# x's lower half turned on TensorE in the place of idle turns, moved waits, and two branches split in four, in a four-layer graph network

## What is computed

```python
x = _layernorm(x + L0(x)); x = _layernorm(x + L1(x)); x = _layernorm(x + L2(x)); x = _layernorm(x + L3(x))
# L0: adj[src, dst] = adj[dst, src] = 1 (a set, not a sum), plus the identity, scaled by deg**-0.5 from both
#     sides; adj @ (x @ weight) + bias
# L1: three convolutions h = A @ (h @ W) + b, where A counts each edge as often as it stands (plus loops)
#     and is scaled by deg**-0.5 from both sides
# L2: q = x @ Wq + bq, k = x @ Wk + bk, v = x @ Wv + bv; a = q @ k.T / sqrt(D), -1e6 where there is no
#     edge; softmax(a) @ v
# L3: h = relu(A @ (x @ W1) + b1); out = A @ (h @ W2) + b2
```

## Time and profile before

| | |
|---|---|
| median of three runs | 546.02 us |
| the profiled execution | 545.62 us |
| its span, first to last instruction | 543.8 us |
| granted clock of TensorE, mean | 0.999 |
| TensorE busy with products | 529.8 us, 97% (2317 instructions) |
| TensorE's weight loads | 373.1 us, 69% |
| VectorE busy | 398.3 us, 73% |
| ScalarE busy | 171.7 us, 32% |
| GpSimd busy | 143.1 us, 26% |

### The profile page before, as it was taken

One profiled execution on the slowest core, in us unless ns is written; L12 is line 12 of the kernel. 1 busy time (PEld: TensorE's weight loads), 2 busy tenths in 40 slices (PEclk: granted clock), 3 DMA queues, 4 the chain that ended last, 5 costly groups with the idle time before them and its releaser, 6 DMA issues.

```text
span 543.8 us, 7062 instructions
## 1 busy us (share of the span) xinstructions
PE 529.8 (97%) x2317; PEld 373.1 (69%) x2317; DVE 398.3 (73%) x873; ACT 171.7 (32%) x361; POOL 143.1 (26%) x135
## 2 busy tenths in 40 slices
PE   8999999999999999999999999899989999999995
PEld 6555565357788888888674764467678888888643
DVE  6888888789878989355576977897887916690165
ACT  5999896472021022220220000542343100120200
POOL 3000000085228504022224800653400390000021
PEclk9999999999999999999999999999999999999999
DMA  8724000100102012000000000000020300000012
GB/s 290 272 79 153 3 1 0 42 1 0 41 9 107 2 19 79 0 1 0 2 1 0 2 0 0 1 0 1 2 77 0 136 0 1 1 1 0 1 58 99
DMA packets 12763, 20.19 MB, mean 37 GB/s; under 512 B 3243, under 2 KB 3507, under 8 KB 12726
## 3 DMA queue, kind: packets, MB, share of 16 engines
q1 hardware_dynamic: 12726, 19.69, 10.7%
HBM read 17.57 MB, written 2.11 MB: 36 GB/s over the span
## 4 chain that ended last, share of the span: by engine, by line
PE 83%; DVE 8%; ACT 4%; issue 3%; POOL 1%; DVEq 0%; POOLq 0%; ACTq 0%
PE bank L951 13%; PE bank L770 13%; PE bank L955 12%; PE bank L788 11%; PE bank L1011 9%; PE bank L844 4%; PE bank L658 3%; PE bank L697 3%; PE bank L643 3%; PE bank L662 3%; PE bank L666 3%; PE bank L983 1%; DVE wk_rows L1519 1%; PE bank L674 1%; ACT apart L1101 1%
## 5 line engine op out<-in xcount | busy, mean ns | idle before, releaser
L549 POOL TENSOR_TENSOR rstd<-veps,mhalf 128x1 f32<-128x1 f32 x32 | 22.2, 695 | 177.5 <-DVE veps L1450 174.7
L1370 DVE TENSOR_TENSOR count<-bank,count 128x160 f32 x128 | 41.3, 323 | 13.9 <-PE bank L697 7.2
L788 PE MATMUL bank<-adj,y_hi 128*128 128x512 f32 x128 | 51.1, 399 | 0.0
L788 PE MATMUL bank<-adj,y_lo 128*128 128x512 f32 x128 | 50.4, 394 | 0.0
L1457 DVE SCALAR_TENSOR_TENSOR xs<-bank,dinv,xs 128x512 f32<-128x512 f32 x23 | 16.9, 746 | 43.9 <-PE bank L844 30.5
L1101 ACT ACTIVATE apart<-col_lo,edge_key 128x128 bf16<-128x128 int16 x128 | 44.0, 395 | 0.7 <-PE bank L686 0.7
L586 POOL TENSOR_SCALAR mask<-count 128x1024 bf16<-128x1024 uint16 x8 | 23.5, 2931 | 52.3 <-DVE peak L1669 43.5
L1354 DVE TENSOR_TENSOR hot_key<-col_key,key 128x320 bf16<-128x320 int16 x128 | 35.4, 316 | 0.2 <-issue 0.2
L697 PEld LDWEIGHTS bank<-hot_key,lo_near 128*128 128x128 bf16 x128 | 12.0, 100 | 31.8 <-issue 23.4
L658 PE MATMUL bank<-w_sb,x0t 128*128 128x512 f32 x64 | 33.1, 601 | 0.6 <-ACT x0t L1082 0.3
L1108 ACT ACTIVATE lo_far<-apart,ones 128x256 bf16<-128x256 bf16 x64 | 31.9, 500 | 0.0
(11 more groups left out here) (288 smaller groups left out, 1241.2 us busy)
## 6 DMA issues: line engine op xcount, KB each, us to landing
w_sb<-in_L_gnn_W_dram SPq DMA_DIRECT2D x3, 1024.0 KB, 5.6
xs<-in_x_dram SPq DMA_DIRECT2D x2, 1024.0 KB, 7.1
v_sb<-in_L_gnn_W_dram SPq DMA_DIRECT2D x2, 1024.0 KB, 6.0
out_dram<-xs SPq DMA_DIRECT2D x7, 256.0 KB, 2.0
w_sb<-in_L_gnn_weight_dram SPq DMA_DIRECT2D x4, 256.0 KB, 6.1
wq_sb<-in_L_gnn_Wq_dram SPq DMA_DIRECT2D x1, 1024.0 KB, 10.6
wk_sb<-in_L_gnn_Wk_dram SPq DMA_DIRECT2D x1, 1024.0 KB, 12.8
wq_rows<-in_L_gnn_Wq_dram SPq DMA_DIRECT2D x1, 1024.0 KB, 7.8
```

The costliest lines, as they stand in the source:

```text
L788: mm = pe.matmul(to, y[part][:, k, f * P:(f + 1) * P], m[:, k, half], start=n == 0 and part == 0 and m is mat, stop=n == NB - 1 and part = ...
L1370: return V.tensor_tensor(count[:, :, bass.ds(at_dst, WIN)], bank[:, slot, n * KEYS:(n + 1) * KEYS].rearrange("p (h d) -> p h d", h=NB), co ...
```

## The change

Four idle turns and eight idle turns go from the opening; in the place of the eight stand the first eight pieces (`TURNED_FIRST`), which are transposes of x's lower half. `EARLY` is three products and sixteen turns, and the pieces of the first "xw" unit stand in another order: its first three products, then the eight turns, then the fourth product. `turn_links(h)` waits for `unit_out` for h = 0, 1 and 2, each for the unit that had its own bank, where h = 0 waited for all. The two If/Else that held whole layers become four, around `cols_steps(2)`, the four `rows_step`s (`layer1_rows`), `cols_steps(10)` and `cols_steps(12)`; the fourteen products of kind "f", those of kind "h" and the last weight products stand between or behind them and are in the program once, not twice. In attention the first score product M1 of pair 2 stands ahead of `turn_probs(0)` on TensorE, `exponents(1)` ahead of `first_part("s", 2)` on ScalarE, `quotients(6)` ahead of `first_mix(2)` on ScalarE, and `reciprocal(6)` ahead of `add_m57(1)` on VectorE.

```diff
--- before.py
+++ after.py
@@ -33,7 +33,8 @@
 WIN = 20
 PAIR = 2
 BY_DVE = 2
-EARLY = 20 * 200 + 2 * 1024
+EARLY = 16 * 200 + 3 * 1024
+TURNED_FIRST = 8
 SHARE = 1280
 TURNED = 200
 SLOTS = 4
@@ -313,7 +314,7 @@
             elif kind == "xw":
                 turns = [(m, k) for m in (n - 2, n - 1) for k in range(4)]
                 if n == 6:
-                    ORDER += [(n, 0), (n, 1)] + turns[:6] + [(n, 2)] + turns[6:] + [(n, 3)]
+                    ORDER += [(n, k) for k in range(3)] + turns + [(n, 3)]
                 else:
                     for k in range(4):
                         ORDER += turns[2 * k:2 * k + 2] + [(n, k)]
@@ -343,7 +344,7 @@
         UA = max(n for n, _ in ORDER[:ALONG]) + 1
         BEHIND = [m for m in range(ALONG, len(ORDER) - 4) if ORDER[m][0] <= UA]
         REST = [m for m in range(ALONG, len(ORDER) - 4) if ORDER[m][0] > UA]
-        assert len(BEHIND) + len(REST) == len(ORDER) - 4 - ALONG and len(REST) == NB
+        assert len(BEHIND) + len(REST) == len(ORDER) - 4 - ALONG and len(REST) == NB and UA % 4 == 3
 
         def unit_bank(n):
 
@@ -686,7 +687,8 @@
                     mm = pe.transpose(bank[:, 2 + n // 2, at_col:at_col + G],
                                       key_rows[:, n, c * P:(c + 1) * P], ident[0:G, 0:G])
                 mm.then_inc(rows_turned, 1)
-            idle_turns(8)
+            for m in range(TURNED_FIRST):
+                piece(m)
             pe.wait_ge(rows_set, 2)
             pe.matmul(bank[:, 0, 0:2 * SPANS * G], ones[0:G, :], group_dia[:].rearrange("g a b -> g (a b)"),
                       start=True, stop=True).then_inc(rows_turned, 1)
@@ -698,8 +700,7 @@
                                  start=c % PAIR == 0, stop=c % PAIR == PAIR - 1)
 
 
-            idle_turns(4)
-            for m in range(*pieces[-1]):
+            for m in range(TURNED_FIRST, pieces[-1][1]):
                 piece(m)
             for g in range(G):
                 pe.wait_ge(win_added, max(2, g + 3 - SLOTS))
@@ -731,8 +732,8 @@
 
             def turn_links(h):
 
-                if h == 0:
-                    pe.wait_ge(unit_out, UA + 1)
+                if h < 3:
+                    pe.wait_ge(unit_out, UA - 2 + h)
                 if h >= 3:
                     pe.wait_ge(sym_max, h - 2)
                 to = bank[:, HALF + h % 3, :].bitcast(BF16)
@@ -955,21 +956,24 @@
                         mm = pe.matmul(to, a[:, k, n * P:(n + 1) * P], b[:, k, :], start=k == 0, stop=k == 1)
                 mm.then_inc(part_done, 1)
 
-            def layer1(mats):
-                more = mats[1] if len(mats) > 1 else None
-                cols_steps(2, adj, yb, NB, more)
-                for n in range(FOLDED):
-                    part(*PARTS[n])
+            def whole_or_apart(steps, rest):
+
+                with pe.If(big < 1):
+                    steps(None)
+                with pe.Else():
+                    steps(rest)
+
+            def layer1_rows(more):
+
                 for half in range(2):
                     rows_step(4 + half, adj, ya1, 2 * NB, more, order=PAIRS)
                 for half in range(2):
                     rows_step(6 + half, adj, yb1, 3 * NB, more)
 
-            with pe.If(big < 1):
-                layer1([adj])
-            with pe.Else():
-                layer1([adj, rest_l1])
-
+            whole_or_apart(lambda more: cols_steps(2, adj, yb, NB, more), rest_l1)
+            for n in range(FOLDED):
+                part(*PARTS[n])
+            whole_or_apart(layer1_rows, rest_l1)
 
             def turn_probs(m):
 
@@ -1027,8 +1031,9 @@
                 for m in names:
                     mix(p, m)
 
+            scores(2, ("M1",))
             turn_probs(0)
-            scores(2, ("M1", "M2", "M6"))
+            scores(2, ("M2", "M6"))
             turn_probs(1)
             mixes(0, ("M1", "M4"))
             scores(2, ("M7", "M5"))
@@ -1054,21 +1059,19 @@
             mixes(2, ("M5", "M7", "M3"))
             mixes(3, MIXES)
 
-            def layer3(mats):
-                more = mats[1] if len(mats) > 1 else None
+            def layer3_first(more):
+
+                if more is not None:
+                    pe.wait_ge(rest_set, 2)
                 cols_steps(10, adj, y3, 4 * NB, more, TILES)
-                for n in range(IN_LAYER2, len(PARTS)):
-                    part(*PARTS[n])
-                cols_steps(12, adj, y3, 5 * NB, more, PAIRS)
-                pe.wait_ge(w_in["v2"], 16)
-                for half in range(2):
-                    weight_step(14 + half, half, by_cols(gt3), v2_sb, 12 + half)
-
-            with pe.If(big < 1):
-                layer3([adj])
-            with pe.Else():
-                pe.wait_ge(rest_set, 2)
-                layer3([adj, rest_l3])
+
+            whole_or_apart(layer3_first, rest_l3)
+            for n in range(IN_LAYER2, len(PARTS)):
+                part(*PARTS[n])
+            whole_or_apart(lambda more: cols_steps(12, adj, y3, 5 * NB, more, PAIRS), rest_l3)
+            pe.wait_ge(w_in["v2"], 16)
+            for half in range(2):
+                weight_step(14 + half, half, by_cols(gt3), v2_sb, 12 + half)
 
         @block.scalar
         def _(act):
@@ -1255,8 +1258,8 @@
             exponents(0)
             quotients(0)
             copy_probs(0)
+            exponents(1)
             first_part("s", 2)
-            exponents(1)
             quotients(1)
             copy_probs(1)
             first_mix(0)
@@ -1275,8 +1278,8 @@
             quotients(5)
             copy_probs(5)
             exponents(6)
+            quotients(6)
             first_mix(2)
-            quotients(6)
             exponents(7)
             copy_probs(6)
             quotients(7)
@@ -1821,8 +1824,8 @@
             m3("s", 3)
             mask_scores(6)
             m4("s", 3)
+            reciprocal(6)
             add_m57(1)
-            reciprocal(6)
             add_m3(1)
             mask_scores(7)
             all_sums(2)
```

## The result

| | before | changed |
|---|---|---|
| median of six runs | 545.81 us | 548.56 us |
| lowest, highest | 545.48, 546.28 | 547.84, 555.24 |
| ratio | | 1.0068, 95% interval 1.0042 to 1.0095 |

Forecast were 546.5 and a range of 542.9 to 547.7. The profiled execution is the slowest of the six, 555.24 us with a span of 553.4, so it shows more than a usual run has to pay. The other five took 547.84 to 549.45.

A forecast was written before the change was run, and what follows sets the result against it. TensorE was taken as nearly always at work, so only its pauses could be saved. Opening 0.5, links 0.7, scores -0.1, tile 6 1.45 and branches -3.0 gave -0.45: 546.5 us at the median, 8-in-10 range 542.9 to 547.7.

The forecast's parts named there:

- Opening: Start and counting: twelve idle turns go, TensorE gets ahead until VectorE limits it; 0.5 us gained, bounds 0 and 1.3.
- what VectorE itself gains: Counting groups 3 and 7, where VectorE now waits for TensorE: 0.2 us of the opening's gain stays.
- x's half could land late: Opening: each 0.1 of late landing delays the counting 0.1, up to 0.5; no separate chance, inside the forecast's range.
- turn_links: First link transposes: no wait for wfold's copy, link slices late next; 0.7 us gained, bounds 0.6 and 0.84.
- Scores: First score product ahead of turn_probs(0): wait moves to turn_probs(1), quotient slightly later; -0.1 us, bounds -0.2 and +0.7.
- Tile 6: turn_probs(6) in attention: earlier quotient lets it start when TensorE is free; 1.45 us gained, bounds 1.1 and 1.6.
- Next late is M1 of pair 3: Behind tile 6: M1's bank is freed by add_m57(2), which comes only 1.1 to 1.5 us earlier.
- Branches: Jumps at 183, 266, 456, 511: code-block pauses cost 1.2, 0.2, 1.6 and 0 us; sum -3.0.
- The new jumps stand where data transfers are few: New jumps: the prediction's argument against the rival that code arrives later.
- Sum: Whole kernel: all terms come to -0.45 us, giving 546.5 at the median, no change that can be told.
- Short jumps cost nothing: New jumps: skipping some 517 instructions, they reach code perhaps held already; gains of 2.35 stand, 543.6 us; chance 0.27.
- Slower: code arrives later: Block behind each target: later code delays 183, 266, 456, perhaps 511; 547.9 us at 0.45 delay; chance 0.17.

The follow-up runs named there:

- e1_again: The changed kernel run once more without an edit: 549.58 us, ratio 1.0077.
- h1_scores_back: e4_shift with the old order at the first scores on TensorE and ScalarE, new opening kept: 543.41 us, ratio 0.9953.
- e4_shift: The changed kernel plus 42 harmless waits in TensorE's stream, moving the four jump targets behind a block's edge: 544.04 us, ratio 0.9969.
- e2_u_later: The changed kernel with SyncE's u_rows transfer held back until four products behind the first new jump are done: 549.19 us, ratio 1.0067.
- h4_u_later_again: e2_u_later run once more without an edit: 548.98 us.
- h2_before_shift: The kernel before with nothing but the 42 extra waits added: 544.32 us, ratio 0.9970.
- h3_two_moves: h2_before_shift plus the links' waits and the moves of quotients(6) and reciprocal(6), both If/Else whole: 542.80 us, ratio 0.9943.
- g1_best: e4_shift with the opening and the first scores' order of the kernel before: 542.91 us, ratio 0.9941.

## Why the prediction was wrong, step by step

- **Opening, forecast 0.5 gained: wrong, and of the wrong sign.** It moved 1.3 us of idle turns out, and the counting ended 0.2 us later (0.28 by the pair above). The lead of TensorE was there at group 0; what I took to stay was "what VectorE itself gains", 0.2, and that came: its adding at group 8 is 0.25 us earlier in e1_again and stays so up to group 48. The other 0.3, from "work moved behind groups 16, 22, 38 and 45", did not. The waits for hot_key rose from 0.6 us in two places to 1.2 to 1.4 in three, and where TensorE is the limit again it had no lead. That x's half could land late stood among the rivals, inside the range; it came in three profiles of nine. The loss is the traces' finding: in time the kernels with and without the new opening have intervals that overlap.
- **turn_links, forecast 0.7: right in kind, 0.3 to 0.5 in size.** The eight transposes do follow the slices, and take 0.80 us for 0.62.
- **Scores, forecast -0.1: right in place, wrong in price.** The wait moved to turn_probs(1), 1.90 us, inside "1.5 to 2", and up to there the changed kernel had lost 0.1 on the kernel before (+9.22 to +9.32). What I did not look for is what lies behind it, the 0.4 us at tile 3 or 1.65 of half clock. The order costs 0.9 us by the ratios of h1_scores_back and e4_shift (intervals that overlap) and about 0.7 by the four profiles without a slow stretch.
- **Tile 6, forecast 1.45: right, 1.3 in size.** The lag fell from 9.95 us ahead of tile 6 to 8.28, and rose again to 8.66 by layer 3, most of that at M1 of pair 3, as the prediction had it ("Next late is M1 of pair 3"). Putting it back cost 1.2 to 1.9.
- **Branches, forecast -3.0: right in place; in size between right and 1.3 short.** Three long jumps more, pauses after so many products and none at the fourth: as drawn. Forecast were three products ahead of the first pause, three ahead of the second and eight turns; four, seven and nine ran. By my recount I had counted labels of the listing as instructions, which they are not; without them the distances are 8, 15 and 22. No run tests that, but the products and turns that ran fit it. Over the old pause the pauses delayed the later work by 2.4 us in e2_u_later and 2.7 in h4_u_later_again (1.9 and 2.2 of it idle time), less than the 3.0. What failed is that a pause was priced at its length: behind the first of them stood a stretch at half clock in three of four profiles, 1.7 to 2.5 us more. "The new jumps stand where data transfers are few" failed too: u_rows was in flight at the first.
- **Sum: the step that failed.** The forecast had the gains at 2.55 us; together they came to 0.1 to 0.3 (e4_shift beside h2_before_shift). Two gains stood, links and tile 6, at 1.5 of their 2.15 (from h2_before_shift to h3_two_moves). The opening and the order at the scores, which I had at +0.4, cost 1.1 to 1.5 (from e4_shift to g1_best): these two terms are most of the miss. The branches cost 4.5 to 5.9 us against the same kernel without pauses; less the old pause's 1.6 or 1.7 that is 2.9 to 4.3 for the 3.0 forecast. With gains of 0.1 and the low end of the branches it is the 2.8 of the result; e1_again with its 3.6 lies further up.
- **Rivals.** "Short jumps cost nothing", which had the most of the chances beside the forecast, is out: every jump over an Else body of 515 to 1,030 instructions takes 3.2 to 3.8 us, and a packet of code starts 0.9 to 1.5 us into each. With it falls the reading of the Trainium skill's figure of 2,048 instructions ("Runtime: NRT & Kernel Launch", section "Instruction fetch mechanics") as what is held ahead; its other rule, that a taken branch out of a window of two blocks must fetch first, agrees with every profile here. It bears on the 3.2 to 3.8 us of the jump, though, and not on the pause, as the prediction took it: the pause is for the block behind the target's, which is moved after the jump has ended (at 266.36 to 267.23 in the kernel before). "Slower: code arrives later" gave 547.9 for a delay of 0.45 at each place; the result lies on its side, but by another way.

## What to carry to other kernels

A forward jump in TensorE's stream was hidden here by the work ahead of it, but only where enough instructions followed its target in the same block of 256 (pauses with 8 to 23 left, none with 32 or more); count that distance in real instructions, and move it with a few harmless ones where it is short. Price a pause of the array with what its clock does behind it, not by its length alone. And take work out of an opening only after asking which engine sets the pace behind it: here that was VectorE up to group 48, and turns that cost nothing were replaced by turns that can be late.

## What the runs showed of the hardware that I had not expected

- Pauses of TensorE of 1.49, 5.68 and 6.67 us at one place were each followed by a stretch at half clock, the one of 0.72 us there was not; a pause of 1.90 us at another place was followed by one in three profiles of nine; the pauses of 1.1 to 1.7 us at the turns of layer 2 by none. It cost 1.6 to 2.5 us. At 1.90 us it differs between executions with the same order there.
- The turns of the opening came at 0.21 us apart, half the pace, until the trace's first record of the clock at 4.75 to 10.34 us, so that the same six turns took 0.87 us in some executions and up to 1.54 in others; the rows give a clock of 1.00 ahead of that record.
- With 512 writes of 4 bytes in flight, TensorE went on only at about their landing, 8.5 and 8.9 us after their issue, though the 16 KB of code it wanted had been moved 4.1 and 6.7 us before; in the two profiles without them the pause was 4 to 6 us shorter.
- Forty-two instructions that wait on a semaphore long reached, seven in a row, cost nothing that the times or the trace show.
